# Second spectral mixer of a four-layer network: the inverse path taken image by image on TensorE, and the routing's relu moved ahead on ScalarE

## The chip, the cores and the metric

The kernel runs on one core of one Trainium2 chip. The metric is the device time of one execution in microseconds (us). Several executions are timed and the median is given; one more execution was recorded by the hardware profiler, and all rows below come from it. Engines are called PE (TensorE, matmuls), DVE (VectorE), ACT (ScalarE), POOL (GpSimd) and SP (the queue that issues DMAs). They run side by side, each works through its own instructions in order, and they hand over by semaphores.

## The reference, cut to what matters

The network has four layers, each a token mixer and a feed-forward part, on an input of 16 images of 16 x 16 tokens with 96 channels. The change touches the mixer of the last layer only (layer normalisation ahead of it, `x` the normalised input):

```python
pooled = x.mean(axis=(1, 2))
h = mlp_scale * jnp.square(jax.nn.relu(pooled @ fc1_w)) + mlp_bias
routeing = jax.nn.softmax((h @ fc2_w).reshape(B, nf, med), axis=1)   # nf = 4, med = 192
xp = act1_scale * jnp.square(jax.nn.relu(x @ pwconv1_w)) + act1_bias
xf = jnp.fft.rfft2(xp, axes=(1, 2), norm='ortho')
...                                   # wc: (16, 9, 4) complex, from a bicubic resize of the weights
weight = jnp.einsum('bfc,hwf->bhwc', routeing, wc)
xo = jnp.fft.irfft2(xf * weight, s=(H, W), axes=(1, 2), norm='ortho')
return xo @ pwconv2_w
```

So two chains run for each image: a small one that makes the routing (pool, two tiny projections, softmax) and with it the spectral weights, and a large one (projection, forward transform, product with the weights, projection back to 96 channels, inverse transform, residual).

## The kernel before, in words

The 4096 tokens lie in on-chip memory in 8 groups of 512 tokens, two images each. A stage is a software pipeline written out by hand: every engine has a function `mixer3(g, p)` that is called for g = -1 to 8 by `mixer_walk` (g = 1 to 4 from a loop, the others unrolled), and what one call, a "body" from here on, issues belongs to up to four groups at once. There is no planner; the order of the calls is the order on the engine. In body g, PE does this, with the names used below:

- **projection** of group g+1 (`mix_h`, lines L1287 to L1289);
- **weights** 0 and 1 of group g (`weights((0, 1))`, L1681), which wait until ACT has copied the spectrum of group g;
- the transposes of the normalised input of group g+2 (`prep_turn`, L1301) and of the routing of group g+1 (`route_turn`, L1667);
- **channels** of group g-1 (`mix_channels`, L1590): 8 matmuls for each of the two images, into one PSUM bank;
- **weights** 2 and 3 of group g, which wait for DVE's first two products (`prod_v`);
- **tokens** of group g-1 (`mix_tokens`, L1603, the inverse transform), which wait for ACT's copy of the channels (`mix_images_out`, L696, semaphore `ps_a`);
- **route_in** of group g+2 (L1653), which waits for DVE's pooled sum (`pl`, L805, semaphore `pool_v`);
- **dft** of group g+1 (`mix_dft`, L1568, the forward transform), 8 matmuls for each image;
- **logits** of group g+2 (`route_logits`, L1661), which wait for DVE's `hh` (L1206, `routing_star`).

ACT in the same body: exp of the routing, two relus of the projection, `mix_star` of image 0 (square and affine, L664 and L667), the high part of the transposed input (L562), `mix_images_out`, `mix_star` of image 1, `routing_hi` (L736), the copy of the spectrum of image 0 (`mix_image`, L684), `routing_relu` (L724 and L726, which wait for route_in), the copy of image 1.

DVE is not touched by the change. The end of its body, in this order, matters below:

```python
if has(g, 0):
    products((2, 3))            # L1254, L1255
if has(g, 1):
    mix_halves(g, 1)            # L1164, L1165: input of the dft of image 1
if has(g, -1):
    mix_x(1, g - 1, xu[6])      # L1169: X += tokens, waits for PE's tokens
if has(g, 1, 2):
    routing_out(g + 1, 1 - p)   # L1227
if has(g, 2, 2):
    routing_star(g + 2)         # L1206: hh, which the logits wait for
```

Ahead of these DVE does: maximum and norm of the routing, products 0 and 1 (they wait for weights 0 and 1), `mix_halves` of image 0, then the low part `XL` (L801) and the pooled sum `pl` (L805) of group g+2. POOL adds the products (L503) and normalises a coming group.

Of the kernel before, what the change touches and what calls it, by code (L numbers as in the profile page):

```python
# [51 lines left out]
def program(nc, a, out):  # L52
    ctx = ExitStack()
    with ctx:
# [8 lines left out]
        def bank(i, n=512, rows=P):  # L63
            return PS[0:rows, i, 0:n]
# [201 lines left out]
        BY_IMAGE = (0, 2, 1, 3)  # L266
# [20 lines left out]
        def has(g, n, least=0, most=GROUPS - 1):  # L287

            return not isinstance(g, int) or least <= g + n <= most

        def after(eng, s, value):

            if not (isinstance(value, int) and value <= 0):
                eng.wait_ge(s, value)
# [12 lines left out]
        def mixer_walk(eng, body, last=GROUPS - 1):  # L307
            walk(eng, body, -1, 1, 4, last)
# [231 lines left out]
        def _(act):  # L540
# [15 lines left out]
            def prep_hi(m, p, ups=None):  # L556
                act.wait_ge(tp_pe, m + 1)
                if ups is None:
                    after(act, xt_used, m - 1)
                else:  # L560
                    act.wait_ge(up_pe, ups)
                act.activation(XH[p][0:C, :], TB, ACT.Copy).then_inc(hi_a, 1)  # L562
# [85 lines left out]
            def mix_relu(kc, k, g):  # L648

                s = 8 * kc + g + 1  # L650
                if kc == 0:
                    after(act, h_v, 2 * s)
                act.wait_ge(h_pe, s + 1)
                for i in range(2):
                    if i == 1:
                        act.wait_ge(xt_used, 8 * k + g + 2)
                    ts = slice(2 * i, 2 * i + 2)
                    act.activation(R[kc][:, ts, :], bank(HB[kc][i], 2 * WID[kc]).rearrange("p (t m) -> p t m", t=2), ACT.Relu)\
                       .then_inc(r_a, 1)

            def mix_star(g, i):
                ts = slice(2 * i, 2 * i + 2)
                act.wait_ge(r_a, 2 * (8 + g + 1) + i + 1)
                act.activation(R[1][:, ts, :], R[1][:, ts, :], ACT.Square).then_inc(sq_a, 1)  # L664
                act.wait_ge(sq_a, 4 * g + 4 + 2 * i + 1)
                after(act, h_v, 2 * (8 + g + 1))
                act.activation(HH[1][:, ts, :], R[1][:, ts, :], ACT.Identity, bias=SBc[1][:, 1:2], scale=SBc[1][:, 0:1])\  # L667
                   .then_inc(sq_a, 1)
# [12 lines left out]
            def mix_image(g, p, i):  # L681
                act.wait_ge(dft_pe, 4 * (8 + g + 1) + 2 * i + 2)
                after(act, prod_v, 8 * g)
                act.activation(XF[1 - p][:, :, :, i, :], bank(SB3[i], 512, C).rearrange("p (c r f) -> p c r f", c=2, r=2), ACT.Copy)\  # L684
                   .then_inc(xf_a, 2)
# [42 lines left out]
            def routing_exp(i):  # L728
                act.wait_ge(rt_v, 5 * i + 3)
                act.activation(le[:], lg[:], ACT.Exp).then_inc(le_a, 1)  # L730
# [18 lines left out]
            def mixer3(g, p):  # L749
                if has(g, 1, 2):  # L750
                    routing_exp(g + 1)
                if has(g, 1):
                    mix_relu(1, 5, g)
                    mix_star(g, 0)
                if has(g, 2, 2, PREPS[6]):
                    prep_hi(40 + g + 2, p)
                if has(g, -1):
                    mix_images_out(g - 1)
                if has(g, 1):
                    mix_star(g, 1)  # L760
                if has(g, 1, 2):
                    routing_hi(g + 1, 1 - p)
                if has(g, 1):
                    mix_image(g, p, 0)
                if has(g, 2, 2):
                    routing_relu(g + 2)
                if has(g, 1):
                    mix_image(g, p, 1)
            mixer_walk(act, mixer3, GROUPS)
            moe(7, 6, 2)  # L770

# [512 lines left out]
        def _(pe):  # L1284
# [290 lines left out]
                                        start=kk == 0, stop=kk == 1)  # L1575
                    ins.then_inc(dft_pe, 1)

            def mix_channels(kc, g, p=0):
                if isinstance(g, int) and g == 0:
                    pe.wait_ge(pad_v, kc + 1)  # L1580
                for i in range(2):
                    if kc == 1:
                        pe.wait_ge(y_p, 4 * g + 2 * i + 2)
                    for n in range(3 - kc):
                        for c in range(2):
                            if kc == 0:
                                o, w = PS[0:C, PB[i], n * C:(n + 1) * C], OU[:, c, i, n * C:(n + 1) * C]
                            else:
                                o, w = PS[:, PB3, (2 * i + n) * C:(2 * i + n + 1) * C], OF[p][:, c, i, n * P:(n + 1) * P]
                            ins = pe.matmul(o, w, PO[kc][:, c, :], start=c == 0, stop=c == 1)  # L1590
                    ins.then_inc(pp_pe, 1)
# [59 lines left out]
            def route_in(i, p):  # L1651
                pe.wait_ge(pool_v, i + 1)
                pe.matmul(TB[0:24, 0:2], fc1[:], pl[:, p, :], start=True, stop=True).then_inc(f1_pe, 1)  # L1653
# [23 lines left out]
            def mixer3(g, p):  # L1677

                def weights(order):
                    for n in order:  # L1680
                        pe.matmul(bank(WB[n], 8 * HF, C), RT[p][:, BY_IMAGE[n], :], CWS[:], start=True, stop=True).then_inc(w_pe, 1)  # L1681
                if has(g, 1):
                    if has(g, 0):
                        pe.wait_ge(xf_a, 32 + 4 * g + 4)
                    mix_h(1, 5, g, p)
                if has(g, 0):
                    pe.wait_ge(rt_x, g + 1)
                    pe.wait_ge(xf_a, 32 + 4 * g + 4)
                    after(pe, prod_v, 8 * g)
                    weights((0, 1))  # L1690
                if has(g, 2, 2, PREPS[6]):
                    prep_turn(40 + g + 2, False, (rt_v, 5 * (g + 1 if has(g, 1) else GROUPS - 1) + 3))
                if has(g, 1, 2):
                    route_turn(g + 1)
                if has(g, -1):
                    if has(g, 1):
                        pe.wait_ge(r_a, 2 * (8 + g + 1) + 2)
                    mix_channels(1, g - 1, 1 - p)
                if has(g, 0):
                    pe.wait_ge(prod_v, 8 * g + 4)  # L1700
                    weights((2, 3))
                if has(g, -1):
                    if not has(g, 0):
                        pe.wait_ge(xu[6], g - 1)
                    mix_tokens(1, g - 1)
                if has(g, 2, 2):
                    route_in(g + 2, p)
                if has(g, 1):
                    mix_dft(1, g)
                if has(g, 2, 2):  # L1710
                    route_logits(g + 2)
            mixer_walk(pe, mixer3, GROUPS)
# [89 lines left out]
```

## Time and profile before

| what | us |
|---|---|
| median of 3 runs | 995.99 (995.64 to 996.19) |
| profiled execution, own time | 994.24 |
| its span, first to last instruction | 992.4 |
| mean granted TensorE clock over the span | 0.923 of full speed |
| the stage of the second spectral mixer (bodies -1 to 8) | 744.4 to 844.3, 99.9 us |
| PE busy over the whole span | 848.9 (86%) |
| DVE, ACT, POOL busy over the whole span | 635.1, 449.3, 565.9 |

Busy shares are averages over stages with different limits, so the stage itself has to be read. PE's clock has two levels, 1.2 and 2.4 GHz; a granted clock of 1.00 in a stretch is the upper one, 0.50 the lower one, and 0.86 is a stretch that had both. The stage falls into the bodies -1 (from 744.41), 0 (754.36), 1 (766.83), 2 (779.38), 3 (790.30), 4 (802.86), 5 (813.79), 6 (824.54), 7 (835.50) and 8 (840.40, up to 844.30, where PE begins the next stage), each taken from the start of PE's first matmul.

### The profile page before, as it was taken

Reading aid. Unit: us, or ns where it says so; the run is one execution under the profiler, and the core shown is the slowest. Engines: PE = TensorE matmul, PEld = TensorE weight load, DVE = VectorE, ACT = ScalarE, POOL = GpSimd, SP = SyncE. Lnnn points to the kernel's source line nnn. Section 1 sums busy time; section 2 is a strip of 40 time slices with the busy share of each in tenths; the row PEclk is TensorE's granted clock in tenths of the full one; section 3 lists DMA queues with packets and bytes.
Section 4 is the critical chain, followed back from the end, with each engine's and each line's share of the span. In section 5 each row is a group of like instructions: output and inputs, shape, how many; then the busy total and the mean of one; then the engine's idle time right before and its main releaser. Section 6 shows DMA issues by size and latency. Waiting matters only on the chain.

```text
span 992.4 us, 24167 instructions
## 1 busy us (share of the span) xinstructions
PE 848.9 (86%) x8782; PEld 701.5 (71%) x8782; DVE 635.1 (64%) x1754; ACT 449.3 (45%) x868; POOL 565.9 (57%) x903
## 2 busy tenths in 40 slices
PE   4766757758878999978999789999958999999997
PEld 4555655747666778867888568888756888688886
DVE  6765678547776565666778625777735776367754
ACT  0433354235555444417677444444314554544441
POOL 5333362134326778775664437868724676677865
PEclk9987779579999999998999989999965999999999
DMA  8500010000012010000000201011000001001020
GB/s 182 100 17 0 1 41 1 1 0 2 0 49 65 27 49 24 26 2 1 1 0 3 62 1 50 26 32 41 2 1 1 1 1 49 26 25 46 27 74 18
DMA packets 39337, 26.58 MB, mean 27 GB/s; under 512 B 27320, under 2 KB 32041, under 8 KB 39201
## 3 DMA queue, kind: packets, MB, share of 16 engines
q1 hardware_dynamic: 38252, 24.64, 9.8%
q8 instruction: 53, 0.87, 0.4%
q10 hardware_dynamic: 998, 0.80, 0.3%
q14 instruction: 34, 0.28, 0.1%
HBM read 8.51 MB, written 1.57 MB: 10 GB/s over the span
## 4 chain that ended last, share of the span: by engine, by line
PE 60%; DVE 14%; issue 9%; ACT 8%; POOL 7%; DMA 1%; ACTq 1%; DVEq 0%; POOLq 0%
PE PS L1513 17%; PE PS L1486 7%; PE PS L1487 6%; PE PS L1490 3%; PE PS L1590 3%; PE PS L1429 3%; PE PS L1611 3%; PE PS L1603 2%; PE PS L1301 2%; ACT H L595 2%; ACT H L677 2%; PE PS L1661 1%; PE PS L1348 1%; PE PS L1287 1%; DVE H L1191 1%
## 5 line engine op out<-in xcount | busy, mean ns | idle before, releaser
L637 ACT ACTIVATE H<-PS,B 128x512 f32<-128x512 f32 x288 | 176.9, 685 | 212.1 <-PE PS L1490 211.5
L1513 PE MATMUL PS<-M,H 128*64 128x96 f32 x4608 | 203.6, 249 | 8.2 <-DVE X L1120 8.2
L1513 PEld LDWEIGHTS PS<-M,H 128*64 128x64 f32 x4608 | 194.8, 139 | 19.1 <-DVE X L1120 8.7
L432 POOL TENSOR_TENSOR msum<-stats 128x4 f32<-128x4 f32 (+1 forms) x61 | 14.2, 233 | 314.3 <-DVE stats L796 277.3
L1120 DVE SCALAR_TENSOR_TENSOR X<-PS,G,X 128x96 f32<-128x96 f32 (+1 forms) x384 | 120.9, 317 | 76.6 <-PE PS L1513 66.0
L1486 PE MATMUL PS<-XH,M1h 128*128 128x512 f32 x192 | 75.7, 395 | 0.0
L1487 PE MATMUL PS<-FHL,M1l 128*128 128x512 f32 x192 | 75.5, 393 | 0.0
L476 POOL TENSOR_TENSOR ex<-euler,dl 128x16 f32<-128x16 f32 x24 | 69.8, 2909 | 7.7 <-DVE dl L1084 7.5
L468 POOL TENSOR_TENSOR PF<-G,B 128x1536 f32<-128x1536 f32 x24 | 66.1, 2756 | 10.1 <-DVE G L1111 10.1
L446 POOL TENSOR_TENSOR rs<-ve,half 128x4 f32<-128x4 f32 (+1 forms) x61 | 66.3, 1086 | 4.8
L1301 PE MATMUL PS<-ident,XN 128*96 128x128 f32 x224 | 39.2, 302 | 21.2 <-DMA WM<-L_conv_b_out 11.9
L1486 PE MATMUL PS<-FHL,M1h 128*128 128x512 f32 x96 | 47.3, 492 | 4.3 <-ACT H L637 4.3
L562 ACT ACTIVATE XH<-PS 96x512 fp32r<-96x512 f32 x56 | 32.9, 587 | 39.9 <-PE PS L1301 39.6
L796 DVE BATCH_NORM_STATS2 stats<-X 128x6 f32<-128x96 f32 (+1 forms) x224 | 41.4, 246 | 14.7 <-DVE G L1111 6.5
L442 POOL TENSOR_TENSOR XN<-X,mean 128x384 f32<-128x384 f32 x56 | 47.5, 848 | 4.1 <-PE PS L1301 4.0
L448 POOL TENSOR_TENSOR XN<-XN,rs 128x384 f32<-128x384 f32 x56 | 47.0, 839 | 4.4
L801 DVE TENSOR_TENSOR XL<-PS,XH 96x512 fp32r<-96x512 f32 x56 | 38.0, 679 | 15.5 <-ACT XH L562 14.8
L1490 PE MATMUL PS<-XL,M1h 32*128 32x512 f32 x288 | 47.8, 491 | 0.0
L1301 PEld LDWEIGHTS PS<-ident,XN 128*96 128x96 f32 x224 | 25.3, 136 | 29.9 <-DMA WM<-L_conv_b_out 11.9
L677 ACT ACTIVATE H<-PS 64x144 f32<-64x144 f32 x128 | 36.4, 284 | 21.2 <-PE PS L1574 19.5
L471 POOL TENSOR_TENSOR PF<-PF 128x768 f32<-128x768 f32 x24 | 43.8, 1823 | 1.9
L503 POOL TENSOR_TENSOR H<-H 96x128 f32<-96x128 f32 x64 | 29.6, 490 | 25.0 <-DVE H L1255 25.0
(246 smaller groups left out, 2006.6 us busy)
## 6 DMA issues: line engine op xcount, KB each, us to landing
FHL<-XH SPq DMA_DIRECT2D x36, 192.0 KB, 2.5
FHL<-XL SPq DMA_DIRECT2D x36, 64.0 KB, 2.2
X<-XH SPq DMA_DIRECT2D x12, 192.0 KB, 2.5
raw<-L_ffn_w SPq DMA_DIRECT2D x3, 576.0 KB, 5.0
M<-L_ffn_w SPq DMA_DIRECT2D x3, 576.0 KB, 6.0
X<-x SPq DMA_DIRECT2D x4, 384.0 KB, 6.7
XH<-XL SPq DMA_DIRECT2D x24, 64.0 KB, 1.9
out<-X SPq DMA_DIRECT2D x8, 192.0 KB, 2.5
```

Source lines behind the costliest of these rows:

```text
L442: pool.tensor_tensor(xn, x, rows(mean), ALU.subtract).then_inc(part, 1)
L446: pool.tensor_tensor(rs[:, 0:n], ve[:, 0:n], half[:, 0:n], ALU.pow).then_inc(part, 1)
L468: pool.tensor_tensor(GB, G[:].unsqueeze(3).to_broadcast([P, GT, EXP, C]), B2[e][:].unsqueeze(1).to_broadcast([P, GT, EXP, C]), ALU.mult).t ...
L476: pool.tensor_tensor(ex[:, :, :].rearrange("p t e -> p (t e)"), euler[:], dl[:, :, :].rearrange("p t e -> p (t e)"), ALU.pow).then_inc(gex ...
L637: act.activation(H[p][:, c, :], bank(UB[c]), ACT.Gelu, bias=B1[e][:, c:c + 1]).then_inc(gelu_a, 1)
L677: ins = act.activation(XP[1 - p][64 * r:64 * r + 64, 2 * c + h, i, :], PS[64 * h:64 * h + 64, DB[j], r * FR:(r + 1) * FR], ACT.Copy)
L1120: ins = dve.scalar_tensor_tensor(xt(g, t), bank(4 + t % 2)[:, e * C:(e + 1) * C], G[:, t, e:e + 1], xt(g, t), ALU.mult, ALU.add)
L1301: ins = pe.transpose(o, XN[:, t, :], ident[:])
L1486: pe.matmul(bank(UB[c]), M1h[e][:, cs], XS[p][j], start=True, stop=False)
L1487: pe.matmul(bank(UB[c]), M1l[e][:, cs], XS[p][k], start=False, stop=False)
L1490: pe.matmul(bank(UB[c]), M1h[e][rows, cs], XL[p][rows, :], start=False, stop=True).then_inc(up_pe, 1)
L1513: ins = pe.matmul(Y[rows, x * C:(x + 1) * C], H[p][:, j, t * P + rows.start:t * P + rows.stop], M2[e][:, j, :], start=c == 0, stop=c == CH ...
```

## The change

Three things move, and nothing is added or removed. On PE, in each body, channels of group g-1 is split by image: image 0 stays, image 1 goes behind weights 2 and 3. Tokens goes behind route_in and behind the first half of dft (the two parts of image 0); the second half of dft follows it. On ACT, `mix_star` of image 1 goes ahead of `mix_images_out`, and `routing_relu` goes ahead of the copies of both images' spectra. DVE, POOL and the DMA queue are untouched.

```diff
@@ ACT, mixer3
+                if has(g, 1):
+                    mix_star(g, 1)
                 if has(g, -1):
                     mix_images_out(g - 1)
-                if has(g, 1):
-                    mix_star(g, 1)
                 if has(g, 1, 2):
                     routing_hi(g + 1, 1 - p)
-                if has(g, 1):
-                    mix_image(g, p, 0)
                 if has(g, 2, 2):
                     routing_relu(g + 2)
                 if has(g, 1):
+                    mix_image(g, p, 0)
                     mix_image(g, p, 1)
@@ PE, mix_channels
-            def mix_channels(kc, g, p=0):
-                if isinstance(g, int) and g == 0:
+            def mix_channels(kc, g, p=0, images=(0, 1)):
+                if isinstance(g, int) and g == 0 and images[0] == 0:
                     pe.wait_ge(pad_v, kc + 1)
-                for i in range(2):
+                for i in images:
@@ PE, mixer3
-                    mix_channels(1, g - 1, 1 - p)
+                    mix_channels(1, g - 1, 1 - p, (0,))
                 if has(g, 0):
                     pe.wait_ge(prod_v, 8 * g + 4)
                     weights((2, 3))
                 if has(g, -1):
+                    mix_channels(1, g - 1, 1 - p, (1,))
+                if has(g, 2, 2):
+                    route_in(g + 2, p)
+                if has(g, 1):
+                    mix_dft(1, g, BY_IMAGE[:2])
+                if has(g, -1):
                     if not has(g, 0):
                         pe.wait_ge(xu[6], g - 1)
                     mix_tokens(1, g - 1)
-                if has(g, 2, 2):
-                    route_in(g + 2, p)
                 if has(g, 1):
-                    mix_dft(1, g)
+                    mix_dft(1, g, BY_IMAGE[2:])
```

On PE, in the loop's body, the order before is this (PO is the weight of channels, CWS that of the spectral weights, the operand pair H,sg is tokens, pl,fc is route_in, sg,H is dft):

```order
L1590 MATMUL PS<-PO,H 128x96 [waits y_p]
L1590 MATMUL PS<-PO,H 128x96 x3
L1583 REGISTER_ALU
L1590 MATMUL PS<-PO,H 128x96 [waits y_p]
L1590 MATMUL PS<-PO,H 128x96 x3
L1700 REGISTER_ALU
L1681 MATMUL PS<-CWS,RT 96x512 [waits prod_v]
L1681 MATMUL PS<-CWS,RT 96x512
L1595 ISA
L1603 MATMUL PS<-H,sg 128x2x96 [waits ps_a]
L1603 MATMUL PS<-H,sg 128x2x96 x3
L1652 REGISTER_ALU
```

The same place after the change (line numbers are one lower there):

```order
L1589 MATMUL PS<-PO,H 128x96 x3
L1699 REGISTER_ALU
L1680 MATMUL PS<-CWS,RT 96x512 [waits prod_v]
L1680 MATMUL PS<-CWS,RT 96x512
L1582 REGISTER_ALU
L1589 MATMUL PS<-PO,H 128x96 [waits y_p]
L1589 MATMUL PS<-PO,H 128x96 x3
L1651 REGISTER_ALU
L1652 MATMUL PS<-pl,fc 24x2 [waits pool_v]
L1561 REGISTER_ALU
L1567 MATMUL PS<-sg,H 96x2x64 [waits h_v]
L1567 MATMUL PS<-sg,H 96x2x64
```

The spectral weights now stand between the images of channels, and route_in with its wait on `pool_v` stands directly behind channels, ahead of tokens.

A few rows further on PE, the order before, from tokens (H,sg) to the forward transform (sg,H):

```order
L1603 MATMUL PS<-H,sg 128x2x96 x3
L1652 REGISTER_ALU
L1653 MATMUL PS<-pl,fc 24x2 [waits pool_v]
L1562 REGISTER_ALU
L1568 MATMUL PS<-sg,H 96x2x64 [waits h_v]
L1568 MATMUL PS<-sg,H 96x2x64
L1568 MATMUL PS<-sg,H 96x2x64 [waits h_v]
L1568 MATMUL PS<-sg,H 96x2x64
```

And after the change:

```order
L1567 MATMUL PS<-sg,H 96x2x64 [waits h_v]
L1567 MATMUL PS<-sg,H 96x2x64
L1594 ISA
L1602 MATMUL PS<-H,sg 128x2x96 [waits ps_a]
L1602 MATMUL PS<-H,sg 128x2x96 x3
L1567 MATMUL PS<-sg,H 96x2x64 [waits h_v]
L1567 MATMUL PS<-sg,H 96x2x64
```

Tokens has moved into the middle of the forward transform, between the two images.

On ACT, in the loop's body, the end of the order before (L696 copies the channels, L664 and L667 are the star of image 1, L736 is `routing_hi`, L684 copies a spectrum, L724 is the routing's relu):

```order
L696 ACTIVATE H<-PS 128x384 [waits id_pe]
L663 REGISTER_ALU
L664 ACTIVATE H<-H 128x384 [waits r_a]
L665 REGISTER_ALU
L667 ACTIVATE H<-H,SBc 128x384 [waits h_v,sq_a]
L733 REGISTER_ALU
L736 ACTIVATE RT<-PS 4x384 [waits w_pe,rt_pe]
L736 ACTIVATE RT<-PS 4x384
L682 ISA
L294 REGISTER_ALU [waits dft_pe]
L684 ACTIVATE H<-PS 96x4x128 [waits prod_v]
L723 REGISTER_ALU
```

And after the change:

```order
L664 ACTIVATE H<-H 128x384 [waits r_a]
L665 REGISTER_ALU
L667 ACTIVATE H<-H,SBc 128x384 [waits h_v,sq_a]
L694 ISA
L695 REGISTER_ALU [waits pp_pe]
L696 ACTIVATE H<-PS 128x384 [waits id_pe]
L733 REGISTER_ALU
L736 ACTIVATE RT<-PS 4x384 [waits w_pe,rt_pe]
L736 ACTIVATE RT<-PS 4x384
L723 REGISTER_ALU
L724 ACTIVATE hr<-PS 24x2 [waits f1_pe]
L725 ISA
```

The star of image 1 now runs before the copy of the channels, and the relu waits for route_in (`f1_pe`) before, not behind, the first spectrum's copy.

## Rows read from the trace of the kernel before

**Rows 1.** The page: span of the profiled execution.

```profile
span 992.4 us, 24167 instructions
```

**Rows 2.** Windows, bodies 1 to 6: length, busy time by engine, granted clock, DMA.

```profile
766.83:779.38 12.55, 11.76 (x83) 10.22 (x82) 8.03 (x26) 6.75 (x15) 7.98 (x20) 0.86 0.01 2
779.38:790.30 10.92, 10.13 (x83) 9.01 (x83) 7.81 (x26) 6.65 (x15) 7.25 (x17) 1.00 0.00 1
790.30:802.86 12.56, 11.77 (x83) 10.44 (x83) 8.29 (x26) 6.64 (x15) 8.68 (x22) 0.86 0.00 0
802.86:813.79 10.93, 10.14 (x84) 9.01 (x83) 7.81 (x26) 6.64 (x15) 7.50 (x17) 1.00 0.00 0
813.79:824.54 10.75, 10.13 (x83) 9.00 (x83) 8.15 (x26) 6.68 (x15) 8.55 (x22) 1.00 0.01 2
824.54:835.50 10.96, 10.02 (x65) 8.89 (x65) 7.47 (x24) 6.43 (x13) 7.92 (x20) 0.84 0.19 54
```

**Rows 3.** Chain of waits, bodies 0 and 4: start, length, engine, tile, line.

```profile
764.64 0.70 DVE hh L1206
765.39 1.51 PE PS L1661 x16
...
811.25 0.34 issue
...
812.01 0.29 DVE hh L1206
812.34 1.51 PE PS L1661 x16
```

**Rows 4.** Timeline of PE, bodies 2 to 7: start, length, instruction, [idle before, releaser].

```profile
788.86 1.51 PE L1661 MATMUL PS<-hh,fc 24*96 24x2 f32 x16 [0.54 <-DVE hh L1206]
...
796.32 0.69 PE L1681 MATMUL PS<-CWS,RT 128*96 128x512 f32 x2
...
805.52 1.95 PE L1590 MATMUL PS<-PO,H 128*128 128x96 f32 x16
807.25 0.69 PE L1681 MATMUL PS<-CWS,RT 128*96 128x512 f32 x2
808.18 1.57 PE L1603 MATMUL PS<-H,sg 128*128 128x192 f32 x8 [0.25 <-ACT H L696]
...
809.82 1.99 PE L1568 MATMUL PS<-sg,H 128*96 128x128 f32 x16
...
823.10 1.51 PE L1661 MATMUL PS<-hh,fc 24*96 24x2 f32 x16 [0.45 <-DVE hh L1206]
...
839.00 1.57 PE L1603 MATMUL PS<-H,sg 128*128 128x192 f32 x8 [0.16 <-ACT H L696]
```

**Rows 5.** Timeline of DVE, bodies 2 to 7, columns as in rows 4.

```profile
784.22 0.68 DVE L805 TENSOR_REDUCE pl<-PS 96x2 f32<-96x512 f32 x1
...
795.04 0.67 DVE L805 TENSOR_REDUCE pl<-PS 96x2 f32<-96x512 f32 x1
...
805.99 0.41 DVE L1255 TENSOR_TENSOR H<-H,PS 96x256 f32<-96x256 f32 x1
...
807.46 0.68 DVE L805 TENSOR_REDUCE pl<-PS 96x2 f32<-96x512 f32 x1
...
809.91 0.54 DVE L1169 TENSOR_TENSOR X<-X,PS 128x384 f32 x1
810.49 0.55 DVE L1227 TENSOR_TENSOR RT<-PS,RT 4x384 fp32r<-4x384 f32 x1
...
818.65 0.67 DVE L805 TENSOR_REDUCE pl<-PS 96x2 f32<-96x512 f32 x1
...
836.98 0.41 DVE L1255 TENSOR_TENSOR H<-H,PS 96x256 f32<-96x256 f32 x1
...
840.60 0.55 DVE L1169 TENSOR_TENSOR X<-X,PS 128x384 f32<-128x384 f32 x1 [0.56 <-PE PS L1603]
```

**Rows 6.** Timeline of ACT, body 7.

```profile
838.45 0.49 ACT L696 ACTIVATE H<-PS 128x384 f32<-128x384 f32 x1 [1.22 <-PE PS L1590]
```

## The prediction, made before the changed kernel was run

> **What bounds the kernel now.** I read the windows of the stage first, then the chain of waits, then the timelines of one body engine by engine. The windows [rows 2] show bodies 1 to 5 with PE busy for all but 0.6 to 0.8 us of each 10.8 to 12.6 us, while DVE is busy for about 8 and ACT for less than 7. So PE sets the pace, and what an order can win is only its gaps. In body 4 the timeline of PE has two: 0.25 us ahead of tokens, which wait for ACT's copy of the channels, and 0.54 us ahead of the logits, which wait for `hh` (rows 4 give the same 0.54 for body 2 and 0.45 for body 5) [rows 4]. The chain of waits says how the second arises: the first image's dft ends, 0.34 us of "issue" (ACT copying the spectrum ahead of the relu), relu and square, `hh` on DVE, logits [rows 3]. The windows also show granted clock 1.00 in bodies 2, 4 and 5 and 0.84 to 0.86 in 1, 3 and 6 [rows 2]: in those the clock was at 1.2 GHz for a part. The same work takes 12.56 us in body 3 and 10.93 in body 4, so one such fall costs 1.6 us [rows 2].
>
> **The change, part by part.** No instruction is added, so PE's busy time stays; each term is a wait that goes, or one that comes.
>
> *The relu ahead of the copies.* It takes the 0.34 us of "issue" out of the path to the logits [rows 3]. `hq` is then ready before the second half of dft has been issued. But `hh` is the last thing of DVE's body, and what stands ahead of it is now late: `mix_x` waits for tokens, then comes `routing_out`, then `hh`. Before, tokens ended ahead of dft and this cost nothing. So what is late next is tokens, moved back by the first half of dft.
>
> *route_in ahead of tokens.* It waits for the pooled sum `pl`. In body 4 `pl` ends at 807.46 + 0.68 = 808.14 [rows 5]. Rows of matmuls end later than their last one is issued: channels take 1.95 us to the end, but the weights start 807.25 - 805.52 = 1.73 behind their start, so the end outlasts the issue by 0.22; the weights, 0.69 long, are thus issued in 0.47 [rows 4]. PE would stand before route_in at 805.52 + 1.73 + 0.47 = 807.72 and wait for `pl` 0.45 us by issue, 0.25 by the ends that the profile counts. That is just what the wait ahead of tokens was (they started at 808.18, with 0.25 idle [rows 4]), and that one is now covered: half of dft is issued in (1.99 - 0.2) / 2 = 0.9 us [rows 4], longer than ACT's copy of 0.49 [rows 6] with its hand-over. Image 1 of channels behind the weights brings another test: weights 2 and 3 wait for DVE's second product, which ends at 805.99 + 0.41 = 806.40 [rows 5], and image 0 of channels is issued at 805.52 + 0.87 = 806.39 [rows 4]. A wait of 0.05 us, inside the wait for `pl`, so nothing.
>
> *From route_in to the logits.* Call the start of route_in R. Tokens and route_in together are issued in 809.82 - 808.18 = 1.64 us, half of dft in 0.9 [rows 4]; the last matmul of tokens ends 0.07 behind its issue and DVE takes over 0.03 later (839.00 + 1.57 = 840.57, `mix_x` begins at 840.60 [rows 4, 5]), so `mix_x` begins at R + 2.64. `routing_out` begins 0.58 later and takes 0.55 (809.91, 810.49 [rows 5]); `hh` takes 0.29 and the logits begin 0.04 behind it (812.01, 812.34 [rows 3]). Sum: logits at R + 4.1. PE itself would be ready at R + 1.64 + 1.8 = R + 3.44, so a gap as long as before, 0.5 us by the ends, is still there, now held by `mix_x` and not by the relu.
>
> Where `pl` decides, R is its end plus 0.05, and the logits come 4.15 us behind the end of `pl` [rows 3 to 5]:
> - body 2: 784.90 + 4.15 = 789.05, before 788.86: +0.2
> - body 4: 808.14 + 4.15 = 812.29, before 812.34: -0.05
> - body 5: 819.32 + 4.15 = 823.47, before 823.10: +0.35
>
> In a body whose channels run at the lower clock, `pl` is early. Body 3: `pl` ends at 795.71 [rows 5], the last weights are issued by 796.32 + 0.47 = 796.8 [rows 4], and as channels and weights only swap, that is R. Logits at 796.8 + 4.1 = 800.9, before about 801.4 (body 4 begins at 802.86 and the logits are issued in 790.30 - 788.86 = 1.44 [rows 2, 4]): -0.5. Body 1 has the same window, 12.55 us at 0.86 [rows 2]: -0.5.
>
> Each body begins when PE has issued its logits, so these terms add.
>
> *The ends of the pipeline.* Body 0 has no channels and no tokens. Its relu stood behind the first copy, `hh` ended at 765.34 and the logits began at 765.39 [rows 3]. Now `hh` is early and the logits follow dft: bounds 0 and -0.5 us (the gap of a steady body), I take -0.3. Body 6 has no route_in; the wait ahead of tokens (0.16 to 0.25 in rows 4) goes: -0.2, bounds 0 and -0.3. Body 7 has neither route_in nor dft. There the weights' issue ran beside ACT's copy of the channels, which ended at 838.94 with tokens at 839.00 [rows 4, 6]; now the weights stand ahead of the last channels and nothing covers the copy. The channels' end moves back by the weights' 0.47, and by 0.1 for the product that ends at 836.98 + 0.41 = 837.39 [rows 5]: +0.6, bounds +0.3 and +0.8. Bodies -1 and 8 issue the same order as before: 0.
>
> Sum: 0.2 - 0.05 + 0.35 - 0.5 - 0.5 - 0.3 - 0.2 + 0.6 = -0.4 us. The profiled execution's own time was 994.24 us with a span of 992.4 [rows 1], so it would be 993.8; the median of the runs is 995.99, and to that I add the sum: **995.6 us, no change that can be measured**. Each term may be off by some 0.2 us, eight together by 0.6, and the modelled ends of matmuls add about as much.
>
> *The clock.* In body 3 the clock fell although the longest wait of PE in the 11 us before was 0.54 us [rows 2, 4]. The Trainium skill, page "TensorE: Matmul & The Clock Gate", section "Why this matters for your kernels", ties a drop in mid-kernel to long idle gaps between bursts of matmuls; by that there would be no fall in this stage, all bodies would run at the upper clock, and my sum would be about 1 us higher, since bodies 1 and 3 would lose their -0.5 each. The trace does not agree. The same page says in Part 4 that a transpose does not count as busy in the way a matmul does, and a body holds two groups of transposes; no row here tells whether they matter, and the change moves none.
>
> What the new order does to the falls can only be bounded. The gaps in a body are as many and about as long as before: one ahead of route_in for one ahead of tokens, and 0.5 ahead of the logits. I take three falls again. One less or one more moves the time by up to 1.6 us [rows 2], a little less in truth, since the new order wins 0.5 in a body with a fall and nothing in one without.
>
> **The rivals.**
> - *Both gaps go.* If the logits were held by the relu alone and `pl` came in time, bodies 1 to 5 would each win 0.25 + 0.54 = 0.79 us, 4.0 in sum [rows 4]; with bodies 0, 6 and 7 (-0.3, -0.2, +0.6) 3.9 us: 992.1. For it speaks that the timeline's waits name just these two, ACT's copy and `hh`. Against it: DVE's order is fixed, and `mix_x` stands ahead of `hh` and waits for tokens, which are issued later than before. Chance 0.12.
> - *One or two falls of the clock less.* A shift by some tenths can let the stage go with one or two stretches at the lower clock. Each one less is worth 1.6 less the 0.5 won in a body with a fall: two less give 2.2 with the sum's 0.4, 993.4; one less gives 994.5, which counts as no change. For it: bodies 2, 4, 5 show that a body need not fall. Against: the gaps are no smaller. Chance of faster by this way 0.10.
> - *Slower: the wait for `pl` feeds the clock's falls.* Place: PE ahead of route_in in bodies 2, 4 and 5. In bodies 2 and 5 it is by 0.2 and 0.35 longer than the gaps it replaces. If that is enough for the clock to fall in these too, each pays 1.6 us less the 0.5 to 0.7 that the new order wins back where the clock falls: 3 x 1.0 = 3, less 0.4: 998.6. It decides from two bodies on. For it: the falls stand in bodies with the same gaps. Against: three of the six full bodies did not fall, with gaps of 0.62 to 0.79 us [rows 2]. Chance 0.12.
>
> **How the numbers follow.** A measurement of this kernel can tell about 0.2%, 2 us, from no change. The forecast and all that lies within 2 us of the time before, one fall more or less included, hold 0.66. Faster by more: 0.12 + 0.10 = 0.22. Slower by more: 0.12. The likeliest case by itself spans 994.0 to 997.2 (the sum's error of 0.9 us, and a part of a fall). The range for 8 in 10 reaches on towards both rivals: 993.2 to 998.0.
>
> **What would show it.** In the profile after, in bodies 2, 4 and 5: (a) no wait ahead of tokens, (b) a wait of 0.25 to 0.5 us ahead of L1652, released by DVE's `pl`, (c) a wait of about 0.5 ahead of the logits, named DVE `hh`, with `mix_x` on DVE now released by PE's tokens and no idle between it and `hh`, and ACT's relu ending more than 1 us ahead of `hh`, (d) bodies of 10.9 to 11.1 us at clock 1.00, of about 12.1 at 0.86, (e) in body 7 a wait of 0.7 us ahead of tokens. The prediction is wrong if the wait ahead of the logits is under 0.2 us in bodies at clock 1.00, if PE does not wait for `pl`, or if the count of bodies with a clock below 1.00 is not three.

## The result, and the profile after

The changed kernel is slower: 1000.65 us in the median of 20 runs, against 995.54 for the kernel before in 20 runs beside it. The medians differ by 5.1 us, and the ratio is 1.0056 with a 95% interval of 1.0039 to 1.0072; 995.6 had been forecast, and the range ended at 998.0. Ratios, here and in the table below, are formed from the fast runs alone and the medians from all runs, so a ratio can differ from the quotient of the two medians, by up to 0.25%.

In the profiled execution (span 999.5 us) the stage of the second mixer runs from 745.40 to 851.35, 105.95 us, where it was 99.89 before. The windows of bodies 1 to 7 of the changed kernel, the last one with body 8 (columns as in [rows 2]):

```profile
767.64:780.25 12.61, 11.58 (x83) 10.52 (x83) 8.58 (x26) 6.91 (x15) 8.40 (x20) 0.86 0.01 2
780.25:792.01 11.76, 10.16 (x84) 9.27 (x83) 8.43 (x26) 6.80 (x15) 8.09 (x19) 1.00 0.00 1
792.01:804.35 12.34, 11.46 (x84) 10.42 (x83) 8.73 (x26) 6.90 (x15) 8.36 (x20) 0.86 0.00 0
804.35:815.86 11.51, 10.03 (x83) 9.26 (x83) 8.44 (x26) 6.79 (x15) 8.09 (x19) 1.00 0.00 0
815.86:828.13 12.27, 11.47 (x83) 10.43 (x83) 8.74 (x26) 6.79 (x15) 8.16 (x20) 0.86 0.01 1
828.13:837.01 8.88, 8.10 (x65) 7.61 (x65) 7.37 (x24) 6.43 (x13) 5.75 (x15) 1.00 0.14 38
837.01:851.35 14.34, 11.15 (x56) 9.90 (x57) 3.97 (x10) 2.85 (x4) 5.80 (x13) 0.76 0.21 61
```

Against [rows 2], bodies 1 to 6 changed by +0.06, +0.84, -0.22, +0.58, +1.52 and -2.08 us. The lower clock has moved from body 6 to body 5: 0.86 in body 5 and 1.00 in body 6, where it was the other way round, and by [rows 2], where a body with such a stretch took 1.6 us more, this is an estimated 1.6 us in each direction. The last window stands out: 14.34 us where bodies 7 and 8 took 8.80 (835.50 to 844.30), at a granted clock of 0.76 where it was 1.00. Bodies 6 to 8 together went from 19.76 to 23.22 us, +3.5; bodies 1 to 5 from 57.7 to 60.5, +2.8. Body 0 gave back 0.2. That is the whole of the stage's 6.1 us. The span is 7.1 us longer; the other 1.0 lies ahead of the stage, where nothing was changed, and the profiles below differ there by more: the stage begins between 740.0 and 748.5 us. So profiles are compared by the stage, and kernels by their medians.

Body 4 is the one to hold against [rows 3 to 5]. PE of the changed kernel (L1589 is channels, L1680 the weights, L1652 route_in, L1602 tokens, L1567 dft, L1660 the logits):

```profile
807.00 1.06 PE L1589 MATMUL PS<-PO,H 128*128 128x96 f32 x8
807.94 0.70 PE L1680 MATMUL PS<-CWS,RT 128*96 128x512 f32 x2
808.48 1.02 PE L1589 MATMUL PS<-PO,H 128*128 128x96 f32 x8
809.68 0.21 PE L1652 MATMUL PS<-pl,fc 96*24 96x2 f32 x2 [0.17 <-DVE pl L804]
809.82 1.11 PE L1567 MATMUL PS<-sg,H 128*96 128x128 f32 x8
810.77 1.47 PE L1602 MATMUL PS<-H,sg 128*128 128x192 f32 x8
812.07 1.04 PE L1567 MATMUL PS<-sg,H 128*96 128x128 f32 x8
814.41 1.51 PE L1660 MATMUL PS<-hh,fc 24*96 24x2 f32 x16 [1.31 <-DVE hh L1205]
```

The wait ahead of tokens is gone and route_in waits 0.17 us for `pl`, as forecast. But the logits wait 1.31 us, not 0.5. DVE at the same time (L804 is `pl`, L1168 `mix_x`, L1226 `routing_out`, L1205 `hh`):

```profile
808.94 0.68 DVE L804 TENSOR_REDUCE pl<-PS 96x2 f32<-96x512 f32 x1
...
812.38 0.56 DVE L1168 TENSOR_TENSOR X<-X,PS 128x384 f32 x1 [0.91 <-PE PS L1602]
812.97 0.55 DVE L1226 TENSOR_TENSOR RT<-PS,RT 4x384 fp32r<-4x384 f32 x1
813.55 0.81 DVE L1205 TENSOR_SCALAR hh<-hq,msb 24x2 f32<-24x2 f32 x1
```

`mix_x` is now released by PE's tokens, and `routing_out` and `hh` follow it without a gap. ACT's relu and square had long ended:

```profile
811.23 0.20 ACT L726 ACTIVATE hq<-hr 24x2 f32<-24x2 f32 x1
```

So the order on DVE holds the logits, as the forecast said. But `hh`, an instruction on 24 partitions and 2 elements, takes 0.81 us, where it took 0.29 in [rows 3]. POOL of the changed kernel, in body 0 and in body 4 (L446 is its power, L448 its multiplication, both part of a group's normalisation):

```profile
764.37 1.04 POOL L446 TENSOR_TENSOR rs<-ve,half 128x4 f32<-128x4 f32 x1
...
813.52 0.82 POOL L448 TENSOR_TENSOR XN<-XN,rs 128x384 f32<-128x384 f32 x1
```

`hh` starts at 813.55, right behind the start of POOL's multiplication (813.52), and ends at 814.36, 0.02 us after it. In body 2 it is the same: `hh` from 789.70 for 0.81. In body 0 `hh` ran beside POOL's power (764.37, 1.04 us) and was not held:

```profile
764.42 0.27 DVE L1205 TENSOR_SCALAR hh<-hq,msb 24x2 f32<-24x2 f32 x1
```

The kernel before had both cases already. These are POOL's multiplications in its bodies 0 and 4:

```profile
764.49 0.82 POOL L448 TENSOR_TENSOR XN<-XN,rs 128x384 f32<-128x384 f32 x1
...
812.18 0.82 POOL L448 TENSOR_TENSOR XN<-XN,rs 128x384 f32<-128x384 f32 x1
```

In body 0 `hh` began at 764.64, 0.15 us into the multiplication, and took 0.70, to 0.02 or 0.03 us behind its end. In body 4 it began at 812.01, 0.17 us ahead of the multiplication, and took 0.29 [rows 3]. In body 4 of the changed kernel it comes 0.03 us behind that start.

The last bodies of the changed kernel, PE from body 7 on:

```profile
837.01 0.68 PE L1680 MATMUL PS<-CWS,RT 128*96 128x512 f32 x2 [0.78 <-DVE RT L1226]
...
838.33 1.03 PE L1589 MATMUL PS<-PO,H 128*128 128x96 f32 x8
841.04 1.17 PE L1680 MATMUL PS<-CWS,RT 128*96 128x512 f32 x2 [1.68 <-DVE H L1254]
842.01 1.86 PE L1589 MATMUL PS<-PO,H 128*128 128x96 f32 x8
844.49 2.93 PE L1602 MATMUL PS<-H,sg 128*128 128x192 f32 x8 [0.63 <-ACT H L696]
847.21 2.18 PE L1589 MATMUL PS<-PO,H 128*128 128x96 f32 x16
```

Weights 2 and 3 stand behind the first image of channels and wait 1.68 us for DVE's products. Behind them everything is at half speed: 8 matmuls of channels take 1.86 us where they took 1.03 in the same body, tokens 2.93 for 1.57. DVE shows why the products are late, and POOL what it waits for:

```profile
839.57 0.42 DVE L1253 TENSOR_TENSOR H<-H,PS 96x256 f32<-96x256 f32 x1 [3.05 <-POOL H L503]
```

```profile
837.76 1.68 POOL L503 TENSOR_TENSOR H<-H 96x128 f32<-96x128 f32 x4
```

DVE waits 3.05 us for POOL's sums of body 6, which end at 839.44. They stand behind POOL's normalisation and end 11.3 us after body 6 began; PE reached body 7 after 8.9. POOL takes up its work of body 6 at 830.81, when DVE's products are there, and has no pause in it longer than 0.1 us until 839.44, so it is POOL's own work that is late, not a wait of POOL.

### The profile page after: what moved, and what is told of

It is laid out like the page before. It is cut to its first block, busy times and chain, and to the rows that moved or that the text cites. A ratio compares the mean times of both kernels' runs of the same rounds, so it can differ in the third digit from the quotient of the medians.

```text
span 999.5 us, 24167 instructions
## 1 busy us (share of the span) xinstructions
PE 851.4 (85%) x8782; PEld 704.9 (71%) x8782; DVE 634.7 (63%) x1754; ACT 450.0 (45%) x868; POOL 566.3 (57%) x903
## 3 DMA queue, kind: packets, MB, share of 16 engines
HBM read 8.51 MB, written 1.57 MB: 10 GB/s over the span
## 4 chain that ended last, share of the span: by engine, by line
PE 59%; DVE 14%; issue 9%; POOL 8%; ACT 7%; DMA 1%; ACTq 0%; DVEq 0%; POOLq 0%
PE PS L1512 16%; PE PS L1485 7%; PE PS L1486 6%; PE PS L1489 4%; PE PS L1428 3%; PE PS L1610 3%; PE PS L1589 2%; ACT H L595 2%; PE PS L1602 2%; PE PS L1300 2%; ACT H L677 2%; PE PS L1347 1%; PE PS L1371 1%; PE PS L1286 1%; DVE H L1190 1%
## 5 line engine op out<-in xcount | busy, mean ns | idle before, releaser
L446 POOL TENSOR_TENSOR rs<-ve,half 128x4 f32<-128x4 f32 (+1 forms) x61 | 66.0, 1081 | 4.8
L448 POOL TENSOR_TENSOR XN<-XN,rs 128x384 f32<-128x384 f32 x56 | 46.4, 828 | 4.4
```

The costliest lines, as they stand in the source:

```text
L446: pool.tensor_tensor(rs[:, 0:n], ve[:, 0:n], half[:, 0:n], ALU.pow).then_inc(part, 1)
```

## The experiments

All times are medians; the kernel before, run beside them, had 995.46 us for e1 to e4, 995.39 for e7 to e10 and 995.26 for e5, e6, e13 and e14. The stage is the profiled stretch from PE's first projection to the next stage; it comes from one execution each, and some of these lie well off their median (e8's took 1001.74 us, e10's 998.86, e13's 984.76).

| run | what it is | us | ratio to before, 95% interval | stage, us |
|---|---|---|---|---|
| after | the change | 1000.65 | 1.0056 [1.0039, 1.0072] | 105.95 |
| e1 | change, body 7 in the old order | 997.03 | 1.0014 [1.0002, 1.0025] | 101.97 |
| e2 | change, another form of hh | 1001.47 | 1.0055 [1.0032, 1.0079] | 105.91 |
| e3 | change, hh ahead of mix_x | 993.29 | 0.9983 [0.9971, 0.9994] | 98.28 |
| e4 | before, relu ahead | 991.60 | 0.9955 [0.9938, 0.9972] | 95.65 |
| e10 | e4, tokens inside dft | 995.73 | 1.0009 [0.9987, 1.0031] | 103.06 |
| e7 | change, POOL's multiplication in 4 | 997.17 | 1.0031 [1.0008, 1.0055] | 101.48 |
| e8 | change, 8 idle matmuls in body 7 | 997.63 | 1.0033 [1.0013, 1.0053] | 103.15 |
| e9 | e4, hh on ACT | 989.51 | 0.9928 [0.9903, 0.9953] | 94.61 |
| e13 | change, e1 and hh on ACT | 989.60 | 0.9925 [0.9895, 0.9956] | 94.46 |
| e14 | e13, route_in behind tokens | 989.01 | 0.9918 [0.9876, 0.9961] | 95.96 |
| e5 | change, e1 and e3 | 988.07 | 0.9905 [0.9873, 0.9937] | 94.42 |
| e6 | PE's part of the change alone | 999.82 | 1.0041 [1.0004, 1.0078] | 105.14 |

**e1: body 7 alone put back.**

```diff
+                tail = isinstance(g, int) and g == GROUPS - 1
...
-                    mix_channels(1, g - 1, 1 - p, (0,))
+                    mix_channels(1, g - 1, 1 - p, (0, 1) if tail else (0,))
...
-                if has(g, -1):
+                if has(g, -1) and not tail:
                     mix_channels(1, g - 1, 1 - p, (1,))
```

> The changed kernel with body 7 alone put back: there PE issues both images of channels, then weights 2 and 3, then tokens, as before. Theory A (the new order of body 7 costs 3 to 4 us, because weights 2 and 3 reach DVE's product 1.7 us early with nothing to cover the wait, and the clock then falls): bodies 6 to 8 together shrink from 23.2 to about 20.5 us and the kernel gains 2.5 to 3 us on the changed one, to about 998. Rival B (POOL's normalisation ends late in body 6, so products, weights and channels of body 7 are late in any order): the wait only moves ahead of weights 2 and 3 or of channels, under 1 us is gained, about 1000.

Measured 997.03, 3.6 us less than the changed kernel. The window of bodies 6 to 8:

```profile
828.93:848.02 19.09, 16.68 (x122) 14.98 (x121) 11.31 (x34) 9.29 (x17) 11.56 (x27) 1.00 0.22 63
```

19.09 us at clock 1.00, where the changed kernel had 23.22 with 0.76 in its larger part. Theory A holds for the cost. Rival B had the cause of the lateness right, though not its price: the products are as late as before (weights 2 and 3 still wait 0.41 us), but the second image of channels now fills most of that wait. The gain is larger than the 3 us expected at most.

**e3: hh ahead of mix_x on DVE.**

```diff
+                if has(g, 2, 2):
+                    routing_star(g + 2)
                 if has(g, -1):
                     mix_x(1, g - 1, xu[6])
                 if has(g, 1, 2):
                     routing_out(g + 1, 1 - p)
-                if has(g, 2, 2):
-                    routing_star(g + 2)
```

> The changed kernel with one thing moved on DVE: hh (routing_star) ahead of mix_x and routing_out. Theory A (the logits are held by hh standing behind mix_x, which waits for tokens): the wait ahead of the logits falls from 0.9 to 1.3 us to under 0.3 in bodies 1 to 5, 4 to 6 us are gained on the changed kernel, about 995. Rival B (the logits are held by route_in's wait for pl and the relu behind it): hh is hardly earlier, under 1 us gained. Rival C (the lower clock is what costs): the waits go but falls of the clock come elsewhere, 1 to 2 us gained.

Measured 993.29, 7.4 us less than the changed kernel and 0.9983 of the kernel before. The logits of bodies 2 and 3 of this kernel:

```profile
787.10 1.51 PE L1660 MATMUL PS<-hh,fc 24*96 24x2 f32 x16
...
797.39 1.51 PE L1660 MATMUL PS<-hh,fc 24*96 24x2 f32 x16
```

No wait stands ahead of them in any body. More was gained than the 4 to 6 us of theory A: only body 1 of bodies 1 to 6 still has a stretch at the lower clock, where the changed kernel had three such bodies. Body 7 still waits 1.68 us here and is followed by its 7 us at the lower clock. Rival B falls, and so does C.

**e2 and e7: why hh is long.** In e2 `hh` has another form, in e7 POOL's multiplication comes in four pieces.

```diff
# e2
-                dve.tensor_scalar(hh[:], hq[:], msb[:, 0:1], msb[:, 1:2], ALU.mult, ALU.add).then_inc(rt_v, 1)
+                dve.scalar_tensor_tensor(hh[:], hq[:], msb[:, 0:1], msb[:, 1:2].to_broadcast([24, 2]), ALU.mult, ALU.add)\
+                   .then_inc(rt_v, 1)
# e7, for this stage's normalisations
-                pool.tensor_tensor(xn, xn, rows(rs), ALU.mult).then_inc(done, 1)
+                if pieces:
+                    for t in range(n):                  # n = 4
+                        ins = pool.tensor_tensor(xn[:, t:t + 1, :], xn[:, t:t + 1, :],
+                                                 rs[:, t:t + 1].unsqueeze(2).to_broadcast([P, 1, C]), ALU.mult)
+                    ins.then_inc(done, 1)
+                else:
+                    pool.tensor_tensor(xn, xn, rows(rs), ALU.mult).then_inc(done, 1)
```

> The changed kernel with hh computed by scalar_tensor_tensor (the bias as a broadcast second tensor) in place of tensor_scalar with two scalars; the same values. Theory A (hh lasts 0.8 us in bodies 2 and 4 because this form of instruction is held while POOL's 0.82 us multiplication runs): hh lasts 0.2 to 0.3 us everywhere, the wait ahead of the logits in bodies 2 and 4 goes from 1.31 to about 0.8 us, and the kernel gains 1 to 2 us. Rival B (hh is long since its input or its place in the queue is late, whatever the form): 0.8 us stays, no change.

> The changed kernel with POOL's multiplication by the reciprocal deviation (L448) cut into 4 instructions of 96 columns in this stage's normalisations, the same values. Theory A (hh is held until the POOL instruction in progress ends, whichever form hh has): no hh lasts over 0.5 us, in bodies 2 and 4 it lasts 0.2 to 0.4 in place of 0.81, the wait ahead of the logits there is 0.8 to 0.95 in place of 1.31, and about 1 us is gained in all, unless POOL's added instructions (some 0.1 to 0.2 us a body) take it back. Rival B (hh waits for something else): 0.81 stays in bodies 2 and 4.

The form of `hh` changes nothing: 1001.47 us, and `hh` still takes 0.80 in bodies 2 and 4 (body 4 of e2):

```profile
813.35 0.80 DVE L1205 SCALAR_TENSOR_TENSOR hh<-hq,msb 24x2 f32<-24x2 f32 x1
```

The cut multiplication does. `hh` and POOL in body 2 of e7 (L450 is the multiplication there):

```profile
790.09 0.33 DVE L1211 TENSOR_SCALAR hh<-hq,msb 24x2 f32<-24x2 f32 x1
```

```profile
790.05 1.25 POOL L450 TENSOR_TENSOR XN<-XN,rs 128x96 f32<-128x96 f32 x4
```

`hh` takes 0.33 us beside a multiplication that takes 1.25 in four instructions. The wait ahead of the logits is 0.83 in bodies 2 and 4, as expected, and the kernel gains 3.5 us by the medians, more than the 1 us expected: the stretch at the lower clock in bodies 7 and 8 is gone (there are some in bodies 1, 3 and 6). The intervals of the two ratios overlap, but 10 of the 12 runs of e7 lie under 999 us and 2 of the 20 of the changed kernel. So `hh` is held until the POOL instruction in progress ends. The Trainium skill states this, page "SBUF — State Buffer", section "Who interferes with whom": DVE and POOL share a pair of ports, which the first to start holds for its whole instruction, and DVE needs it in its two-port modes or with two inputs from on-chip memory. By that section `tensor_scalar`, the form of the changed kernel, can enter such a mode, and the form of e2 has two inputs, which fits e2. The traces agree where `hh` met POOL's multiplication (0.81 us), and where it met POOL's sums or subtraction it also took longer, up to 0.54 (bodies 1, 3 and 5 of the changed kernel) and 0.71 us (e3). They do not agree for POOL's power on 128 x 4 elements, which did not hold `hh` in body 0 (0.27 us beside 1.04, and 0.20 in the form of e2) or in bodies 2 and 4 of e4; why stays open.

**e4, e10 and e6: the parts alone.** e4 is the kernel before with the relu ahead of both copies. e10 is e4 with tokens inside dft. e6 is PE's part of the change with ACT as before.

```diff
# e4
-                if has(g, 1):
-                    mix_image(g, p, 0)
                 if has(g, 2, 2):
                     routing_relu(g + 2)
                 if has(g, 1):
+                    mix_image(g, p, 0)
                     mix_image(g, p, 1)
# e10, added to e4
+                if has(g, 2, 2):
+                    route_in(g + 2, p)
+                if has(g, 1):
+                    mix_dft(1, g, BY_IMAGE[:2])
                 if has(g, -1):
                     if not has(g, 0):
                         pe.wait_ge(xu[6], g - 1)
                     mix_tokens(1, g - 1)
-                if has(g, 2, 2):
-                    route_in(g + 2, p)
                 if has(g, 1):
-                    mix_dft(1, g)
+                    mix_dft(1, g, BY_IMAGE[2:])
```

> The kernel before with one part of the change: on ACT the routing's relu ahead of both copies of the spectrum; PE's order and the star stay as before. Theory A (before the change hh waited for the relu alone, and mix_x was done early): the wait ahead of the logits falls from 0.54 to about 0.2 us, 1.5 to 2.5 us faster than before, about 993.5. Rival B (hh then meets POOL's long multiplication and is held by it): no change or up to 1 us slower.

> The kernel with the relu alone moved (991.6 us in the run before) plus one thing: tokens between the two halves of the forward transform, route_in ahead of them; channels, weights and the star stay in the old order, body 7 too. Theory A (the loss in bodies 1 to 5 comes from tokens alone, because DVE's mix_x, routing_out and hh wait for them in that order): the wait ahead of the logits is 0.8 to 1.3 us again in bodies 1 to 5, and the time is 4 to 6 us above the relu alone, about 997. Rival B (the split of channels around the weights costs it): the time stays within 1 us of the relu alone, about 992.

> PE's part of the change alone: ACT as before, with the copy of the channels ahead of the star of image 1 and the relu between the two copies of the spectrum. Theory A (the relu's place does not matter once hh stands behind mix_x, and the star has slack): within 1 us of the changed kernel, about 1001. Rival B (the star behind the copy of the channels now comes late for the second half of the forward transform): a wait ahead of that half, 1 to 4 us above the changed kernel.

The relu alone gives 991.60, ratio 0.9955: 3.9 us faster than before, more than expected. Not all of it is the shorter wait: in its profile bodies 3 and 6, which had a stretch at the lower clock before, have clock 1.00. The logits of bodies 2 and 3 in e4, PE and DVE:

```profile
789.38 1.51 PE L1660 MATMUL PS<-hh,fc 24*96 24x2 f32 x16
...
800.41 1.51 PE L1660 MATMUL PS<-hh,fc 24*96 24x2 f32 x16 [0.64 <-DVE hh L1205]
```

```profile
788.96 0.27 DVE L1205 TENSOR_SCALAR hh<-hq,msb 24x2 f32<-24x2 f32 x1
...
799.60 0.75 DVE L1205 TENSOR_SCALAR hh<-hq,msb 24x2 f32<-24x2 f32 x1
```

In body 2 `hh` takes 0.27 us and PE does not wait; in body 3 it starts 0.09 behind POOL's multiplication (799.51), takes 0.75, and PE waits 0.64. Both theories are thus seen in one trace, A in bodies 1, 2 and 4, B in 3 and 5. e10 brings the waits ahead of the logits back (0.90, 1.31, 0.77, 0.77 and 0.46 us in bodies 1 to 5) and 4.1 us with them: tokens inside dft, behind route_in, is what costs in the steady bodies, without any split of channels. e6 lies 0.8 us below the changed kernel: PE's part by itself is the loss, and the relu's place, worth 3.9 us in the old order in e4, is worth nothing in the new one. Rival B of e6 is seen in part: in bodies 5 and 6 the second half of dft waits 0.73 and 0.98 us for DVE's halves, which waited for the star. Against that the waits ahead of the logits in bodies 1 to 5 are shorter by 0.4 to 0.6 us each, and the 7 us at the lower clock begin at the end of body 5 and not in body 7.

**e8: what the clock costs at the end.**

```diff
+                if isinstance(g, int) and g == GROUPS - 1:
+                    for _ in range(8):
+                        pe.matmul(bank(3, 8 * HF, C), RT[p][:, 0, :], CWS[:], start=True, stop=True)
                 if has(g, 0):
                     pe.wait_ge(prod_v, 8 * g + 4)
                     weights((2, 3))
```

> The changed kernel with 8 extra matmuls of 512 columns into a free PSUM bank in body 7, behind the first image of channels, where PE waits 1.68 us for DVE's product; their results are not used. They take 8 x 0.22 = 1.8 us at the upper clock. Theory A (the fall of the clock at the end of the stage comes from PE's waits there and costs some 3 us): no fall or one of half the length in bodies 7 and 8, the stage is 2 to 3 us shorter although PE does more. Rival B (the waits themselves are the loss): the stage is as long or up to 0.3 us longer, with the fall still there.

Measured 997.63, 3.0 us less than the changed kernel, with more work on PE (9 of its 12 runs lie under 999 us, though the intervals of the ratios overlap). Its profiled execution took 1001.74 us, but what it lost lies ahead of the stage, which begins 3.1 us later than in the changed kernel. The window of bodies 7 and 8 of e8:

```profile
840.10:851.60 11.50, 9.98 (x64) 8.40 (x65) 3.93 (x10) 2.86 (x4) 5.83 (x13) 1.00 0.24 70
```

11.50 us at clock 1.00, against 14.34 at 0.76. PE's 1.68 us of waiting is filled, nothing else is altered, and 2.8 us are gone. Of the 4.1 us by which e1 shortens bodies 6 to 8 in its profile, about two thirds are thus the clock and one third the waits; by the medians the clock's part is 3.0 of 3.6. That the fall hangs on the wait is seen in the other runs too: e2 and e3, which keep the wait of 1.68 us, keep 7 us at the lower clock behind it, and e1 and e7, with waits of 0.41 and 0.96, have none there.

**e9, e13, e14 and e5: both causes taken away.** e9 is e4 with `hh` on ACT. e13 is the changed kernel with body 7 put back and `hh` on ACT, e14 the same with route_in behind tokens, e5 is e1 and e3 together.

```diff
# e9, e13, e14
                 act.activation(hq[:], hr[:], ACT.Square).then_inc(rt_a, 1)
+                act.wait_ge(rt_a, 2 * i + 2)
+                act.activation(hh[:], hq[:], ACT.Identity, bias=msb[:, 1:2], scale=msb[:, 0:1]).then_inc(rt_v, 1)
...
-                dve.wait_ge(rt_a, 2 * i + 2)
-                dve.tensor_scalar(hh[:], hq[:], msb[:, 0:1], msb[:, 1:2], ALU.mult, ALU.add).then_inc(rt_v, 1)
# e14 also
-                if has(g, 2, 2):
-                    route_in(g + 2, p)
                 if has(g, 1):
                     mix_dft(1, g, BY_IMAGE[:2])
                 if has(g, -1):
                     ...
                     mix_tokens(1, g - 1)
+                if has(g, 2, 2):
+                    route_in(g + 2, p)
```

> The kernel before with the routing's relu ahead of both copies, and hh computed on ACT behind the square instead of on DVE. Theory A (with the relu alone moved, hh on DVE is held by POOL in bodies 3 and 5, which leaves waits of 0.64 and 0.43 us ahead of the logits): no wait ahead of the logits in any body, 0.5 to 1.5 us faster than the relu alone, about 990.5. Rival B (the logits then wait for ACT or the clock falls more): within 0.5 us of the relu alone or slower.

> The changed kernel with both suspected causes taken away: body 7 in the old order, and hh computed on ACT behind the square, so that it waits neither for mix_x nor for POOL. Theory A (these two are all that is wrong with the new order): no wait ahead of the logits in bodies 1 to 5, the only wait there is route_in's for pl (0.17 to 0.56 us), bodies of 10.1 to 10.4 us, kernel about 989 to 990, 11 us faster than the changed kernel and level with the old order plus relu and hh on ACT (989.5). Rival B (something else in the new order costs, such as route_in's wait): 991 or more.

> As e13, with route_in behind tokens again, so that it does not wait for pl. Theory A: bodies 1 to 5 have no wait of PE over 0.2 us, about 10.0 us each at the upper clock, kernel about 988. Rival B (relu, square and hh behind a later route_in now come late for the logits): a wait of 0.1 to 0.3 us ahead of the logits takes back what the pl wait cost, 989 to 990.

> The changed kernel with hh ahead of mix_x on DVE (993.3 alone) and body 7 in the old order (997.0 alone). Theory A (the two causes lie in different bodies and add): 7.4 + 3.6 = 11 us below the changed kernel, 989 to 990.5. Rival B (both work through the clock's falls and share them): 991 to 993.

All four beat both kernels: 989.51, 989.60, 989.01 and 988.07 us. Theory A holds in e9 (2.1 us under e4, no wait ahead of the logits), e13 and e5. e5 is 12.6 us below the changed kernel, where e1 and e3 alone give 3.6 and 7.4, 11.0 in sum, and its stage is 11.5 us shorter, where they give 4.0 and 7.7: the two causes lie in different bodies and add. A steady body of e5, between its two first projections:

```profile
788.25:798.54 10.29, 9.85 (x83) 9.19 (x82) 8.50 (x26) 6.80 (x15) 7.86 (x20) 1.00 0.00 0
```

10.29 us at clock 1.00, against 10.92 in [rows 2]. e9, in the old order of PE, reaches the same, since 0.25 us ahead of tokens is all that PE still waits for there. e14 has no wait for `pl` but one of 0.28 to 0.33 ahead of the second half of dft in bodies 2, 4 and 5, which is neither theory's: PE is now ahead of DVE's halves of image 1. Its interval overlaps those of the other three, so between these orders the runs do not decide.

## Why the prediction was wrong

*Right.* PE bounds the stage. The wait ahead of tokens goes in the steady bodies, and route_in waits for `pl` instead (0.16 and 0.17 us in bodies 2 and 4, 0.25 forecast). The relu ends over 1 us ahead of `hh`, and `hh` is held by `mix_x`, which waits for tokens; e3, e10 and e4 show that this is the cause. Body 0 gave 0.2 of 0.3, and tokens in body 7 wait 0.63 us, 0.7 forecast. So the gain that the relu's place brings by itself, 3.9 us in e4, is lost to the new order of PE.

*Wrong in size: "`hh` takes 0.29".* The row was taken from a body in which `hh` began 0.17 us ahead of POOL's multiplication (812.01 against 812.18). In the new place `hh` meets that multiplication and takes 0.81 in bodies 2 and 4, and 0.54 and 0.39 beside POOL's sums in bodies 1 and 3. The waits ahead of the logits were 0.88 to 1.31 us there, not 0.5, and bodies 2 and 4 lasted 11.76 and 11.51, not 10.9 to 11.1. The logits came 4.8 us behind the end of `pl` in bodies 2 and 4, not 4.15, and 4.56 behind R in body 1, not 4.1. Bodies 1 to 4 were forecast at -0.85 us in sum and measured +1.26. Of these 2.1 us the longer `hh` is 1.4 (0.25, 0.52, 0.10 and 0.52); the rest is small lateness all along the way that no run takes apart. e7 shows that the POOL instruction is the reason for bodies 2 and 4. The same row had its warning beside it: in [rows 3] `hh` took 0.70 in body 0.

*Wrong, the term for body 7: "by 0.1 for the product that ends at 836.98 + 0.41 = 837.39".* That end was taken over from a trace in which body 6 lasted 10.96 us, mostly because it had a stretch at the lower clock. In the changed kernel body 6 lasted 8.88, and then it is POOL that ends last: the sums behind its normalisation end 11.0 us after the start of body 6 in the kernel before and 11.3 in the changed one. DVE's products begin 11.44 us after it in both, released by PE's weights before and by POOL after. The weights waited 1.68 us. Two runs with the same order in body 7 bear this out: in e7 body 6 had a stretch at the lower clock and lasted 10.50, and the weights waited 0.96; in e6 it lasted 12.86, and they did not wait. The forecast for bodies 6 to 8 was +0.4, measured +3.5. This is the largest step of the miss: 3.1 us, against 2.1 in bodies 1 to 4 and 1.2 in body 5, which has the lower clock that body 6 had before.

*Wrong: "I take three falls again".* Bodies 1 to 6 have three again, 1, 3 and 5. But the waits at the end brought a fourth, of 7 us, in bodies 7 and 8; by e8 it costs 2.8 us. So five bodies had a clock below 1.00, which by the prediction's own last sentence makes it wrong. The rival that had the clock fall more often (998.6) put it ahead of route_in in bodies 2, 4 and 5. Bodies 2 and 4 kept clock 1.00 with 1.5 us of waits each, and the waits for `pl` there were 0.16 and 0.17 us. It named the right sign and about half the size, but neither the wait nor the place.

## What to carry to other kernels

When an instruction is freed from one wait, read what stands ahead of it on its own engine, and what the engine that can hold it (here POOL) runs at its new time; a duration of 0.3 us from a quiet moment is no price for a busy one. Give the drain of a pipeline its own budget, counted from the engine that ends last there, since the work that covers a wait in the steady bodies is missing there, and a wait of 1.7 us cost 2.8 us more through the clock here. Take no end time over from a trace in which the body before had another clock. Try the parts of a change alone: here the relu's place was worth 3.9 us by itself, and the rest of the change, put on top of it, took 9.

## What the runs showed of the hardware

An instruction of DVE on 24 x 2 elements took 0.81 us when it began just behind the start of POOL's multiplication on 128 x 384 elements (0.82 us), ending 0.02 behind it, in either form tried; on ACT the same operation took 0.39 in every body (e9). Beside POOL's power on 128 x 4 elements (1.04 us) it took 0.27: the power did not hold it. Eight matmuls whose results nobody uses, 1.9 us of PE's time inside a wait, saved 2.8 us by keeping the granted clock at its upper level. The clock fell less often where the waits ahead of the logits were gone. Of bodies 1 to 6, e3, e5, e9 and e13, with none of these waits, had one with a stretch at the lower clock each, and e14 two; the kernel before, with 0.45 to 0.54 us in each body, and the changed kernel, e1, e2, e7 and e8, with 0.66 to 1.31, had three, and e6 and e10 four; e4, with such waits in two bodies only, had one. Each count is from one execution. What decides on the body stays open. In the changed kernel the stretches begin 1.1 to 1.6 us into bodies 1, 3 and 5, those of bodies 3 and 5 thus behind the waits of 1.31 us at the end of bodies 2 and 4; but in the kernel before one begins in body 3 and none in body 2, behind the same wait of 0.54.
